# Cross-attention in a two-layer decoder: scores as one pass of 96 contraction rows, and the values product as one matmul a key chunk with high and low parts side by side

## The reference

```python
def _L0_xattn_ref(query, bank, Wq, bq, Wk, bk, Wv, bv, Wo, bo):     # 16 heads of 32
    q = split_heads(query @ Wq + bq)                                 # 8, 16, 100, 32
    k = split_heads(bank @ Wk + bk)                                  # 8, 16, 722, 32
    v = split_heads(bank @ Wv + bv)
    scores = jnp.einsum('bhqd,bhkd->bhqk', q, k) / scale
    attn = jax.nn.softmax(scores, axis=-1)
    out = jnp.einsum('bhqk,bhkd->bhqd', attn, v)
    return out.transpose(0, 2, 1, 3).reshape(B, -1, D) @ Wo + bo
```

## Time and profile before

| | us |
|---|---|
| median of three runs | 2616.84 |
| lowest, highest | 2612.31, 2621.23 |
| span of the profiled execution | 2613.8 |
| TensorE busy | 2432.4 (93% of the span) |
| VectorE busy | 1110.8 (42%) |
| ScalarE busy | 947.7 (36%) |
| GpSimd busy | 585.1 (22%) |
| share of the DMA engines, mean | some 10% |

### The profile page before, as it was taken

One profiled execution on the slowest core, in us unless ns is written; L12 is line 12 of the kernel. 1 busy time (PEld: TensorE's weight loads), 2 busy tenths in 40 slices (PEclk: granted clock), 3 DMA queues, 4 the chain that ended last, 5 costly groups with the idle time before them and its releaser, 6 DMA issues.

```text
span 2613.8 us, 38193 instructions
## 1 busy us (share of the span) xinstructions
PE 2432.4 (93%) x14208; PEld 2160.2 (83%) x14208; DVE 1110.8 (42%) x2206; ACT 947.7 (36%) x1892; POOL 585.1 (22%) x397
## 2 busy tenths in 40 slices
PE   4899999999977789699999999998999999999997
PEld 3788888888866667588888888887999999999997
DVE  7455545555457368444556455654640000200022
ACT  2444434454443144343454344533222222311130
POOL 4111101110132634311111011101222222222222
PEclk9899999999978878789999999998999999999998
DMA  3000000000021010100100000000111111111111
GB/s 136 1 24 24 15 8 23 23 23 6 22 81 29 1 44 0 60 1 28 28 27 21 6 27 27 32 1 33 64 48 65 56 64 56 56 56 64 56 57 41
DMA packets 29513, 93.60 MB, mean 36 GB/s; under 512 B 3752, under 2 KB 4008, under 8 KB 29320
## 3 DMA queue, kind: packets, MB, share of 16 engines
q1 hardware_dynamic: 29448, 92.72, 11.0%
HBM read 91.07 MB, written 1.64 MB: 35 GB/s over the span
## 4 chain that ended last, share of the span: by engine, by line
PE 86%; DVE 6%; ACT 3%; POOL 3%; issue 2%; DMA 0%; DVEq 0%; SPq 0%; POOLq 0%; ACTq 0%
PE psS L272 18%; PE psS L274 16%; PE psS L273 16%; PE psT L1337 7%; PE psJ L272 4%; PE psJ L273 4%; PE psJ L274 4%; PE psO L272 4%; PE psO L274 3%; PE psO L273 3%; PE psT L272 2%; PE psT L274 2%; PE psT L273 2%; DVE x_res L884 1%; DVE stats L877 1%
## 5 line engine op out<-in xcount | busy, mean ns | idle before, releaser
L272 PE MATMUL psS<-hid_hi,fw_hi 128*128 128x400 f32 x1152 | 398.1, 346 | 15.4 <-DVE hid_lo L1258 10.6
L274 PE MATMUL psS<-hid_hi,fw_lo 128*128 128x400 f32 x1152 | 400.2, 347 | 0.0
L273 PE MATMUL psS<-hid_lo,fw_hi 128*128 128x400 f32 x1152 | 399.6, 347 | 0.0
L529 POOL TENSOR_TENSOR fw_lo<-raw,fw_hi 128x1024 fp32r<-128x1024 f32 x88 | 216.7, 2464 | 572.1 <-ACT fw_hi L751 572.1
L615 ACT ACTIVATE pT_hi<-psT 128x300 fp32r<-128x300 f32 x512 | 187.4, 418 | 263.0 <-PE psT L1337 262.5
L1258 DVE TENSOR_TENSOR hid_lo<-h_act,hid_hi 128x800 fp32r<-128x800 f32 x32 | 32.3, 1083 | 555.6 <-ACT hid_hi L840 555.6
L606 ACT ACTIVATE p<-psS,nmax 100x722 f32<-100x722 f32 x256 | 221.9, 867 | 68.9 <-DVE nmax L928 36.4
L936 DVE TENSOR_TENSOR pT_lo<-psT,pT_hi 128x300 fp32r<-128x300 f32 x512 | 216.4, 464 | 38.1 <-ACT pT_hi L615 32.8
L370 POOL TENSOR_TENSOR cT_lo<-ctx_raw,cT_hi 128x722 fp32r<-128x722 f32 x58 | 102.1, 1761 | 580.0 <-ACT cT_hi L565 580.0
L272 PEld LDWEIGHTS psS<-hid_hi,fw_hi 128*128 128x128 f32 x1152 | 218.0, 189 | 16.4 <-issue 11.2
L272 PE MATMUL psO<-pT_hi,vv_hi 128*64 128x200 f32 (+1 forms) x768 | 219.2, 285 | 2.4 <-DVE oraw L947 2.4
(11 more groups left out here) (306 smaller groups left out, 4909.4 us busy)
## 6 DMA issues: line engine op xcount, KB each, us to landing
raw<-ffn_dram SPq DMA_DIRECT2D x88, 512.0 KB, 3.2
ctx_raw<-ctxT_dram SPq DMA_DIRECT2D x60, 361.0 KB, 3.1
mask_raw<-mask_dram SPq DMA_DIRECT2D x8, 282.0 KB
raw<-wk_dram SPq DMA_DIRECT2D x4, 512.0 KB, 3.5
raw<-wv_dram SPq DMA_DIRECT2D x4, 512.0 KB, 6.6
raw<-wq_dram SPq DMA_DIRECT2D x4, 512.0 KB, 3.3
raw<-wo_dram SPq DMA_DIRECT2D x4, 512.0 KB, 3.2
cin<-xT_dram SPq DMA_DIRECT2D x1, 1600.0 KB, 8.3
```

The source lines that it names most:

```text
L272: nc.tensor.matmul(out, st[0], mv_[0], start=first, stop=False)
L273: nc.tensor.matmul(out, st[0], mv_[1], start=False, stop=False)
L274: return nc.tensor.matmul(out, st[1], mv_[0], start=False, stop=last)
L529: nc.gpsimd.tensor_tensor(fw.lo[:, e, :], raw[:, e, :], fw.hi[:, e, :], ALU.subtract)\
```

## The change

- **Scores.** The three passes become one. A stack `kS` holds for each head 96 rows: hi, lo and hi of its keys, one below the other; `qS` holds hi, hi and lo of its queries. One matmul of 96 contraction rows gives the sum of the three products: two matmuls a head instead of six.
- **How the stacks are filled.** SyncE copies each 32-row part of each head from `kT` to `kS` by DMA: 12 copies a group (`key_stack`). The queries are split on VectorE as they are made (`queries_split`), written to DRAM three times a unit (`queries_out`), and loaded from there into `qS`, three DMAs a group (`query_stack`). `q_all`, `queries_hi` on ScalarE and `queries_lo` on GpSimd go. Both stacks have two buffers; `kT` has one now, and ScalarE's first half of a group waits until the stack before has landed.
- **Keys.** By `KEYS_AT` they are made in steps 1 and 2 (group 2), 7 and 8 (group 3), 14 and 15 (next batch's group 0), and group 1 of the next batch in the tail.
- **Values product.** `vv` and `pT` hold hi and lo side by side. One matmul of 128 stationary columns (two heads, hi and lo) and 400 moving columns (hi and lo of both heads' probabilities) a chunk: three matmuls a step for nine. The useful blocks of `psO` are now four a head: VectorE sums two (`heads_out`, a reduce), ScalarE copies the cross one (`heads_cross`, tile `ocross`), and one more VectorE addition a batch brings them together (`o_summed`).
- **Context.** The third and fourth context copies come in steps 12 and 13, not 13 and 14.
- **Bias rows.** `rows` holds one of three bias rows at a time; each is loaded when the one before has been used.

```diff
-CONTEXT_AT = {10: 0, 11: 1, 13: 2, 14: 3}
+CONTEXT_AT = {10: 0, 11: 1, 12: 2, 13: 3}
+KEYS_AT = {1: (0, 2, 0), 2: (0, 2, 1), 7: (0, 3, 0), 8: (0, 3, 1), 14: (1, 0, 0), 15: (1, 0, 1)}
...
-        vv = pair("vv", [P, NKC, D])
+        vv = at("vv", [P, NKC, H, 2, HD], f32r)
...
-        kT = pair("kT", [P, 2, KEYS])
+        kT = pair("kT", [P, KEYS])
...
+        kS = at("kS", [STACK * HD, 2, G, KEYS], f32r)
...
-        pT = pair("pT", [P, 2, NKC, 2 * T])
-        qs = pair("qs", [P, C, T])
+        pT = at("pT", [P, 2, NKC, 2, 2 * T], f32r)
+        qS = at("qS", [STACK * HD, 2, G, T], f32r)
         oraw = at("oraw", [P, C, T], fp32)
+        ocross = at("ocross", [P, C, T], fp32)
...
+            def queries_out(L):
+
+                a = A[L]
+                for i in range(2 * C):
+                    m, h = i // 2, i % 2
+                    sp.wait_ge(a.q_lo, i + 1)
+                    for part, t in enumerate((q_parts.hi, q_parts.hi, q_parts.lo)):
+                        sp.dma_start(q_dram[L][h * NB // 2:(h + 1) * NB // 2, m, part].rearrange("b j r t -> (j r) b t"),
...
+            def query_stack(L, b, g):
...
+                wait(sp, a.s_mm, H * b + G * (g - 1))
+                for part in range(STACK):
+                    sp.dma_start(qS[HD * part:HD * (part + 1), g % 2, :, :].bitcast(fp32),
+                                 src[:, g, part].rearrange("a j r t -> r (a j) t"))\
+                      .then_inc((a.stack0, a.stack1)[g % 2], 16)
+
+            def key_stack(L, b, g):
+
+                a = A[L]
+                sp.wait_ge(a.k_lo, 8 * b + (2 * g + 2))
+                for part, t in enumerate((kT.hi, kT.lo, kT.hi)):
+                    for j in range(G):
+                        sp.dma_start(kS[HD * part:HD * (part + 1), g % 2, j, :].bitcast(fp32),
+                                     t[HD * j:HD * (j + 1), :].bitcast(fp32))\
+                          .then_inc((a.stack0, a.stack1)[g % 2], 16)
...
+                def batch(b, last):
+                    if not last:
+                        context(a, b + 1, range(2))
+                    for g in range(2, C):
+                        query_stack(L, b, g)
+                        key_stack(L, b, g)
+                    if not last:
+                        context(a, b + 1, range(2, C))
...
+                        for g in range(2):
+                            query_stack(L, b + 1, g)
+                            key_stack(L, b + 1, g)
...
-            def queries_lo(a, b):
...
-            def queries_hi(a, b):
...
                 act.wait_ge(a.k_mm, 8 * b + 2 * g + i + 1)
-                dst = kT.hi[:, g % 2, k0:k0 + kn]
+                if i == 0:
+                    wait(act, (a.stack0, a.stack1)[(g + 1) % 2], GROUP_IN * (2 * b + (g + 1) // 2))
+                dst = kT.hi[:, k0:k0 + kn]
...
+                def heads_cross(b, pr):
+
+                    act.wait_ge(a.pv_mm, H // 2 * b + pr + 1)
+                    if pr == 0:
+                        wait(act, a.o_summed, b)
+                    for e in range(2):
+                        g, j = divmod(2 * pr + e, G)
+                        cp = nc.scalar.activation(ocross[HD * j:HD * (j + 1), g, :],
+                                                  psO[2 * HD * e + HD:2 * HD * (e + 1), T * e:T * (e + 1)], ACT.Copy)
+                    cp.then_inc(a.o_crossed, 1)
...
+                        if t >= 4 and t % 2 == 0:
+                            heads_cross(b, (t - 4) // 2)
...
+            def queries_split(L):
+
+                a = A[L]
+                for i in range(2 * C):
+                    dve.wait_ge(a.q_done, i + 1)
+                    wait(dve, (a.q_out0, a.q_out1)[i % 2], 48 * (i // 2))
+                    nc.vector.tensor_copy(q_parts.hi[:, i % 2, :], qf[:, i % 2, :]).then_inc(q_hi, 1)
+                    dve.wait_ge(q_hi, 2 * C * L + i + 1)
+                    nc.vector.tensor_tensor(q_parts.lo[:, i % 2, :], qf[:, i % 2, :], q_parts.hi[:, i % 2, :],
+                                            ALU.subtract).then_inc(a.q_lo, 1)
...
-                        cp = nc.vector.tensor_copy(oraw[HD * j:HD * (j + 1), g, :],
-                                                   psO[HD * e:HD * (e + 1), T * e:T * (e + 1)])
+                        r = slice(2 * HD * e, 2 * HD * e + HD)
+                        cp = nc.vector.tensor_reduce(oraw[HD * j:HD * (j + 1), g, :],
+                                                     psO[r, 0:4 * T].rearrange("p (s x t) -> p x t s", s=2, x=2)[:, e],
+                                                     AX.X, ALU.add)
...
+                    nc.vector.tensor_tensor(oraw[:, :, :], oraw[:, :, :], ocross[:, :, :], ALU.add)\
+                      .then_inc(a.o_summed, 1)
...
-                        pe.wait_ge(a.k_lo, 8 * b + 2 * g + 2)
+                        pe.wait_ge((a.stack0, a.stack1)[g % 2], GROUP_IN * (2 * b + g // 2 + 1))
...
-                        mm = three(psS[h % 2][0:T, k0:k0 + kn], (qs.hi[rows_, g, :], qs.lo[rows_, g, :]),
-                                   (kT.hi[rows_, g % 2, k0:k0 + kn], kT.lo[rows_, g % 2, k0:k0 + kn]), True, True)
+                        mm = nc.tensor.matmul(psS[h % 2][0:T, k0:k0 + kn], qS[:, g % 2, j, :],
+                                              kS[:, g % 2, j, k0:k0 + kn], start=True, stop=True)
...
-                        mm = three(psO[0:2 * HD, 0:2 * T], (vv.hi[0:n, k, fs], vv.lo[0:n, k, fs]),
-                                   (pT.hi[0:n, pr % 2, k, :], pT.lo[0:n, pr % 2, k, :]), k == 0, k == NKC - 1)
+                        mm = nc.tensor.matmul(psO[:, 0:4 * T],
+                                              vv[0:n, k, 2 * pr:2 * pr + 2, :, :].rearrange("p h s e -> p (h s e)"),
+                                              pT[0:n, pr % 2, k, :, :].rearrange("p s t -> p (s t)"),
+                                              start=k == 0, stop=k == NKC - 1)
...
-                        for j in range(3, NKC):
-                            values(a, b + 1, j)
+                        values(a, b + 1, 3)
+                        values(a, b + 1, 4)
+                        keys(a, b + 1, 1, 0)
+                        values(a, b + 1, 5)
+                        keys(a, b + 1, 1, 1)
```

More of the change, by code:

```diff
@@ L106, in decoder_kernel @@
         resid = at("resid", [T, 2, D], fp32)
-        rows = at("rows", [T, 3, D], fp32)
+        rows = at("rows", [T, D], fp32)
         sel = at("sel", [H, C, P], fp32)
@@ L200, in decoder_kernel @@
         silu, gated = at("silu", [P, 2, HALF], fp32), at("gated", [P, 2, HALF], fp32)
+        q_dram = [nc.dram_tensor(f"q_dram{L}", (NB, C, STACK, G, HD, T), fp32, kind="Internal").ap() for L in range(2)]
         def ps(name, n):
@@ L316, in _ @@
+                with nc.sync.Fori(0, NB - 1) as b:
+                    batch(b, False)
+                batch(NB - 1, True)
             sp.dma_start(cols[:, :], d["cols"]).then_inc(conv_in, 16)
@@ L625, in batch @@
                             exps(b, t)
-                        g, i = t // 4 + 1, t % 4
-                        if i < 2 and g < C and t < 12:
+                        if t >= 4 and t % 2 == 0:
+                            heads_cross(b, (t - 4) // 2)
+                        ahead, g, i = KEYS_AT.get(t, (2, 0, 0))
+                        if ahead == 0:
                             keys_hi(L, b, g, i)
-                        if t >= H - 1 and not last:
-                            keys_hi(L, b + 1, 0, t - H + 1)
+                        if ahead == 1 and not last:
+                            keys_hi(L, b + 1, g, i)
                         if t in CONTEXT_AT and not last:
@@ L639, in batch @@
                     if not last:
-                        queries_hi(a, b + 1)
                         values_hi(a, b + 1, 0)
+                    heads_cross(b, H // 2 - 1)
+                    if not last:
                         values_hi(a, b + 1, 1)
@@ L690, in _ @@
             queries(A[0], True)
-            act.wait_ge(A[0].q_done, 2 * C)
-            queries_hi(A[0], 0)
+            for i in range(2):
+                keys_hi(0, 0, 1, i)
             for i in range(2):
@@ L809, in _ @@
             queries(A[1], False)
-            act.wait_ge(A[1].q_done, 2 * C)
-            queries_hi(A[1], 0)
+            for i in range(2):
+                keys_hi(1, 0, 1, i)
             for i in range(2):
@@ L960, in batch @@
                             norm_apply(base + b - 1, 0, y[:, 0, :], b - 1)
-                        g, i = t // 4 + 1, t % 4
-                        if i < 2 and g < C and t < 12:
+                        ahead, g, i = KEYS_AT.get(t, (2, 0, 0))
+                        if ahead == 0:
                             keys_lo(L, b, g, i)
-                        if t >= H - 1 and not last:
-                            keys_lo(L, b + 1, 0, t - H + 1)
+                        if ahead == 1 and not last:
+                            keys_lo(L, b + 1, g, i)
```

(18 more changed lines are left out.)

127 lines of the change are left out of this document (75 added, 52 removed).

## The result

The changed kernel takes 2670.76 us (median of 4 runs, 2661.39 to 2673.15) against 2618.2 before: a ratio of 1.0192, 95% interval 1.0169 to 1.0214. It is slower by some 50 us (1.92% of 2618.2). Its profiled span is 2667.8 us, 54.0 more than the 2613.8 before.

A forecast was written before the change was run, and what follows sets the result against it. TensorE, 93% busy, was taken as the bound, with the exp loop of about 2.5 us a step right under it. 14 periods saved 43 us, last batches 4, starts cost 34: 13 us faster, about 2604, range 2555 to 2680.

The forecast's parts named there:

- the second rival: Clock falls in steps without keys, 1.6 falls a batch, a step 3.3 us: 55 us slower, 2670; chance 0.25.
- the clock's: Attention batches: a clock fall costing 4.6 us in 6 of 10 batches, adding 2.8 us a period; bounds none to three.
- at full clock, with no wait for a stack: Batch period: 43.3 us first to last transpose, 2.2 and 0.8 for added VectorE and ScalarE work, 30.6 at the end.
- late stacks: ScalarE's step 1 and head 12's scores wait for DMA-filled key stacks: 0.9 us a batch, bounds 0 and 5.
- signs of being wrong: Batch periods below 77 or above 84 us, or stack copies landing more than 9 us after the subtraction.
- the third rival: Key stacks land late at head 12 and ScalarE's step 1, 3.5 us a batch more: 35 us slower, 2652; chance 0.15.
- The Trainium skill's rule: Key-stack copies: 32 partitions reach half the DMA ports, about 5 us a stack, or 10 if reads and writes met.
- Steps without keys: Attention steps without key matmuls go from 2.65 to 2.5 us, where the exp loop ends the wait.
- the reduces: VectorE output copies become two reduces over 200 elements, estimated 0.36 us each.
- the end of a batch: From a batch's last transpose to the next batch's first: 30.7 us before, forecast 30.6.
- Start of the layers: Queries split, written to DRAM and read back before scores: 17 us more a layer, 34 in all; bounds 10 and 30.
- The 400-byte writes: Query writes to DRAM at layer start: 200 KB landing 2.5 us plus queueing; if twice as slow, about 6 us more a layer.

The follow-up runs named there:

- x1: Changed kernel with each stack filled by 4 copies of 96 partitions instead of 12 of 32, same bytes but rows not the heads' own: 2626 us, ratio 1.0028 to before.
- x2: Changed kernel with each score matmul issued three times in steps without keys from step 3 on, all over 96 rows: 2644 us, ratio 1.0096 to before.
- x10: Changed kernel, key group 3 and next batch's group 1 made earlier, scores repeated, extra matmuls before head 1's scores, first two context copies one step earlier: 2603 us.
- x4: Kernel before with only the values half of the change (one 400-column matmul a chunk), scores still in three passes: 2673 us, ratio 1.0227.
- x7: Kernel before with three overwritten 512-column matmuls ahead of the scores of heads 1 and 3, batches 0 to 6 of each layer: 2576 us, ratio 0.9828.
- x12: Changed kernel with the high part of the queries written to DRAM once and read twice, 16 writes a layer instead of 24: 2660 us, ratio 1.0166 to before.
- x5: Changed kernel with the edits of x1 (4 copies a stack) and x2 (repeated score matmuls) together: 2611 us, ratio 0.9966 to before.
- x6: As x2, but the two repeated score passes cover 32 contraction rows and only the third covers 96: 2690 us, ratio 1.0260 to before.

## Why the prediction was wrong

Forecast 2604, range 2555 to 2680, chance of slower 0.37. The time lies inside the range, on the other side of no change. It is what the second rival gave (2670, chance 0.25), the clock that falls in the steps without keys.

**The step that failed** is the clock's: "I take a fall of today's size (4.6 us) in 6 of 10 batches", a term of 2.8 us a batch. Measured are two or three falls in nearly every batch, 14 to 27 us of half clock in each full period but the first, at a cost of some 5.4 us a batch. That cost is an estimate from the timelines: each step (from its first transpose to the next step's), in the mean over the 14 periods, less the same step where the clock was 1.00 and no stack was waited for (in the changed kernel, x1, x2 or x10). By it the mean period of 84.9 us is

| us a batch | forecast | measured |
|---|---|---|
| at full clock, with no wait for a stack | 76.9 | 77.5 |
| late stacks (steps 2 and 12) | 0.9 | 2.0 |
| half clock | 2.8 | 5.4 |
| sum | 80.6 | 84.9 |

The first row has a check: three periods of x10 in layer 0 have no half clock, and they take 77.8 to 78.5 us. Of the 60 us by which the 14 periods were off, the clock is some 36, the stacks 16 and the rest 9. That the clock is a cost, and not only a sign, x2 shows (26 us come back by adding work); x4 that one half of the change suffices for it, x7 that even the old kernel paid 44 us for it. The text had the evidence: it said that the fall stands right behind steps with scores and transposes only, and then thinned nine steps a batch to about that and gave this a quarter of the chance. One of its own signs of being wrong, periods above 84 us, came true.

**The second miss** is the stacks': 0.42 us an issue and 7.1 us a stack, 0.9 us a batch. Measured are 0.63 apart, 9.0 us, and waits of 2.6 and 1.7 us: inside the bounds given (0 to 5), far off the value taken. The batch pays 2.0 of them by the table, since a part of each wait would otherwise be a wait for the exponentials. By x1 the late stacks are worth 44 us of the kernel, with what they do to the clock. The issue durations shown were all of copies that read DRAM; a copy that reads and writes SBUF behind another of its kind takes 0.59 to issue. This was the third rival's mechanism, at 1.1 us a batch more in place of its 3.5, the clock apart. So the second rival's number came out right by luck, with another make-up: a clock cost of 5.4 in place of its 7.4 us a batch (a step at half clock takes 3.00 us, not the 3.3 it gave), and 1.1 us more for the stacks and 0.6 more at full clock than it had.

The Trainium skill's rule from "SBUF — State Buffer", section on the DMA port swizzle, by which 32 partitions reach half of the ports, was not what made the stack late: one copy of 90 KB lands in 2.1 us, as interpolated, and the copies are issued 0.63 us apart with each issue taking 0.59. x1 moved the same bytes in 96-partition copies of 3.6 to 3.9 us landing each. The stack's time is the queue's.

**What held.** Steps without keys 2.48 us (2.5), with TensorE waiting 0.84 for the exponential (0.85); the reduces 0.36 us each (0.36); the end of a batch 634.76 less 604.12, its last transpose, 30.6 us (30.6). Start of the layers: 20.4 and 16.6 us; 17 each were forecast. The 400-byte writes landed in 4.0 and 4.7 us (2.5 assumed, plus queueing). The first of each layer, with no write ahead of it, landed in 2.9 (issues at 87.07 and 1139.54), later ones in up to 5.8, and x12 took 4.9 us off with eight writes fewer; so a part of it is that they stand behind each other. The Trainium skill says in "DMA: Bandwidth & Descriptors", Specifications, that below 512 bytes the engines do read-modify-write; no run here has the same bytes in longer pieces, so what that costs is not shown, and the 6 us a layer that doubled writes would have added did not come in layer 1 and at most in part in layer 0.

**Missed:** `psO` waits of 1.1 us (step 9) and 1.3 (step 15), where the reduces stand behind a key subtraction; the text put them ahead of the exponentials only. They are 2.4 us a batch, in the steps at full clock above; other terms of those were taken too long, so that 0.6 is left.

The changed kernel's 54 us of span, then: 37 for the starts; 3 more in layer 0's last batch; from layer 1's last batch start on 3 less (6.0 in the batch, against 2.8 more behind it, not looked into); 17 in the periods. These are 84.9 us in the mean; x10, with stacks early, TensorE filled and two context copies moved, has 80.1, 3.6 less than the kernel before. Of the 4.8 between, x1 gives 2.9 (with its share of the clock) and x2 2.4 (the stacks still late); together, in x5, they give 4.0, less than their sum: x1's TensorE waits longer for the exponentials, x2's for the stack.

## What to carry to other kernels

Before taking work off TensorE next to a loop of another engine, look at the granted clock by step: where it falls behind thin steps, a change that thins more steps can cost more than it saves, and matmuls into a buffer that is about to be overwritten are a cheap test (and here a cheap remedy, 44 us). Take care when reading that test: filling gives back what the clock costs less what the next limit takes (x2: 26 us, with the stacks still late). Price a chain of DMAs by its issues on the queue, with the issue duration of the same kind of copy, and by how late the last one lands. A buffer that is copied by DMA makes its next writer wait for the whole copy; count what stands behind that writer.

## What the runs showed that was not expected

- With two of three score passes over 32 contraction rows instead of 96, same columns, the mean granted clock went from 0.95 to 0.90 and the kernel took 46 us more (x6 against x2). So what the clock follows is not TensorE's busy time alone; x4 fell from full clock at 12.23 of 12.60 us busy. What it does follow no run here shows.
- A DMA issue takes 0.32 to 0.36 us in the median on SyncE's queue for the query, context and feed-forward loads from DRAM and 0.59 for key copies within SBUF, in the same kernel; the number of partitions (32 or 96) made next to no difference to it (0.59 and 0.60 in x1).
- Once down, the clock stayed at half for up to 10.2 us in a period before, 13.7 in the changed kernel and 20.4 in x4, through stretches in which TensorE was busy 12.20 of 13.70 us (changed) and 20.35 of 20.40 (x4).
